# Routing in two halves, routed tiles in the same program as the shared chunks, and the first shared chunk at step 16

## The reference

```python
x = x + xattn(ctx, ctx, layernorm(x), Wv, Wk, Wq, Wo, bo)
x = x + ffn(layernorm(x), ...)

def ffn(x, ...):                      # xf: 2048 x 256
    sh = gelu(einsum('nd,sdh->snh', xf, sw1) + sb1)          # 2 shared experts, 512 wide
    shared_out = (einsum('snh,shd->nd', sh, sw2) + sb2.sum(0)) / 2
    gates = xf @ router_w + router_b                          # 8 experts
    topv, topi = top_k(gates, 2); probs = softmax(topv)
    h = gelu(einsum('nd,edh->enh', xf, w1) + b1)
    y = einsum('enh,ehd->end', h, w2) + b2
    return shared_out + sum over the 2 chosen experts of probs * y
```

## Time and profile before

| | us |
|---|---|
| median of 3 runs (lowest, highest) | 382.54 (381.79, 382.92) |
| the profiled execution | 382.79 |
| its span, first to last instruction | 381.1 |
| PE busy | 332.8 (87%) |
| DVE busy | 234.7 (62%) |
| ACT busy | 222.6 (58%) |
| POOL busy | 201.2 (53%) |
| mean granted clock of PE | 0.957 |

### The profile page before, as it was taken

The page is one execution under the profiler, slowest core; times in us unless marked ns, Lnnn a source line. Parts: engine busy times, 40 slices in busy tenths (PEclk is TensorE's granted clock), DMA queues, the critical chain, the costliest instruction groups (busy, mean ns, idle before and its releaser), DMA issues. The chain is left out here.

```text
span 381.1 us, 8081 instructions
## 1 busy us (share of the span) xinstructions
PE 332.8 (87%) x2297; PEld 279.3 (73%) x2297; DVE 234.7 (62%) x483; ACT 222.6 (58%) x405; POOL 201.2 (53%) x238
## 2 busy tenths in 40 slices
PE   5979989877678999989799658999999999999970
PEld 4757666645457888969689535898999999999860
DVE  0589999999734429694455232565666666566650
ACT  1265567865749646646456414666667676776650
POOL 4326799999737900387377210335554445445542
PEclk9998999998989999999899957999999999999997
DMA  8960000060006201047552643245544544554332
GB/s 267 399 237 1 3 0 31 28 236 0 3 0 233 101 1 57 27 144 211 160 183 88 207 128 135 33 69 85 82 67 78 83 75 72 85 84 63 53 42 28
DMA packets 23929, 36.92 MB, mean 97 GB/s; under 512 B 4400, under 2 KB 18096, under 8 KB 23504
## 3 DMA queue, kind: packets, MB, share of 16 engines
q1 hardware_dynamic: 16000, 25.06, 20.4%
q0 software_dynamic: 7456, 10.04, 15.4%
q10 hardware_dynamic: 432, 1.31, 1.0%
HBM read 23.21 MB, written 13.19 MB: 96 GB/s over the span
## 5 line engine op out<-in xcount | busy, mean ns | idle before, releaser
L945 POOL DMA_INDIRECT out<-y,xg x39 | 61.0, 1564 | 68.6 <-DVE y L1009 51.6
L691 DVE TENSOR_TENSOR h_lo<-g,h_hi 128x512 fp32r<-128x512 f32 x32 | 24.4, 764 | 51.4 <-PE psS L855 26.2
L1063 PE MATMUL ps<-w_lo,hh_hi 128*128 x156 | 47.1, 302 | 3.5 <-DVE hh_lo L1015 3.5
L996 DVE TENSOR_TENSOR hb<-ps,b1T 128x512 f32<-128x512 f32 x39 | 27.0, 691 | 36.5 <-PE ps L1052 36.0
L855 PE MATMUL psS<-s_lo,h_hi 128*128 128x256 f32 x128 | 37.8, 295 | 9.5 <-DVE h_lo L691 9.5
L1063 PE MATMUL ps<-w_hi,hh_lo 128*128 x156 | 44.0, 282 | 0.0
L1063 PE MATMUL ps<-w_hi,hh_hi 128*128 x156 | 43.6, 280 | 0.0
L487 ACT ACTIVATE g<-psP,sb1T 128x512 f32<-128x512 f32 x32 | 22.0, 687 | 34.6 <-PE psP L841 34.5
L381 POOL TENSOR_TENSOR Pr<-Pr,inv 128x1024 f32<-128x1024 f32 x16 | 30.4, 1902 | 19.1 <-DVE inv L682 19.1
L970 ACT ACTIVATE g<-hb 128x512 f32<-128x512 f32 x39 | 24.7, 632 | 26.9 <-DVE hb L996 26.9
L855 PE MATMUL psS<-s_hi,h_lo 128*128 128x256 f32 x128 | 36.9, 288 | 0.0
(11 more groups left out here) (181 smaller groups left out, 913.1 us busy)
## 6 DMA issues: line engine op xcount, KB each, us to landing
wraw<-in_w SPq DMA_DIRECT2D x16, 512.0 KB, 5.7
xg<-xg_d SPq DMA_DIRECT2D x39, 130.0 KB, 2.4
sraw<-in_sw SPq DMA_DIRECT2D x2, 1024.0 KB, 11.0
out<-xres SPq DMA_DIRECT2D x4, 512.0 KB, 3.5
xres<-in_x SPq DMA_DIRECT2D x3, 512.0 KB, 9.5
xTs<-in_xT SPq DMA_DIRECT2D x3, 512.0 KB, 10.1
xg_d<-filler SPq DMA_DIRECT2D x8, 128.0 KB
b_bc<-in_b SPq DMA_DIRECT2D x1, 1024.0 KB, 6.0
```

The costliest lines, as they stand in the source:

```text
L691: V.tensor_tensor(out=h_lo[:, n % 2], in0=g[:, n % 2], in1=h_hi[:, n % 2].bitcast(F32), op=ALU.subtract).then_inc(hlo_done, 1)
L945: pool.indirect_dma_start(out, bass.IndirectOffsetOnAxis(ap=xg[:, t % NXB, D:D + 1].bitcast(U32), axis=0), y[:, t % NYB], None, compute_op ...
L996: V.tensor_tensor(out=hb[:, n % 2], in0=ps[:, 4 + n % 2].rearrange("p (c n) -> p c n", c=HC), in1=b1T[:, bass.ds(e, 1), :].squeeze(1).unsq ...
L1063: last = nc.tensor.matmul(ps[:, 6 + n % 2, 0:D], a[:, n % 2, c], b[:, bass.ds(e, 1), C * HF + c * D:C * HF + (c + 1) * D].squeeze(1), star ...
```

## The change

`front` and `routed_experts` become one function, `program`, with one block of engine programs.

- FIRST_CHUNK is 16. Chunks 0 and 1 stand in the last steps of attention. hidden(n) is now written after output(n-2) in step n, so the order of those two on PE is as before. PE's x2 transposes (L795 before) stand ahead of the Wo product (L788 before) in a step.
- The chunks' hidden parts use two banks of `psS`, the outputs the other two and `psP`. The routed tiles use the chunk's buffers and banks again, with waits on the last chunk's semaphores.
- Routing runs for tiles 0 to 7 (gates at n = 0 and 1, slots at 4) and for tiles 8 to 15 (7, 8 and 11). Tables stand at n = 12 to 14. POOL scatters four groups of eight.
- All low parts are made by DVE, at the n of a table (LOWS), the high parts by ACT at those of HIGHS.
- DVE's additions of a constant to the variance, and the negated mean, are tensor_tensor with a constant column (`eps`, `minus`) in SBUF instead of tensor_scalar with an immediate.
- SP: the store of group 1 comes after expert 5; seven `xg` tiles are loaded ahead of the last stores instead of three.
- `x_transpose(0)` and `(1)` stand at chunks 29 and 30, and the last two outputs between the first routed tiles.

```diff
-FIRST_CHUNK = NT + 2
+FIRST_CHUNK = NT
-EARLY = 3
+EARLY = 7
+SPLIT_X = {5: 1, 10: 2, 18: 3}
+HIGHS = {2: 2, 3: 2, 4: 2, 6: 2, 7: 1, 8: 2, 9: 2, 11: 2, 12: 2, 13: 2, 14: 1, 17: 2, 19: 2, 22: 2, 23: 2, 25: 2, 26: 2}
...
+        h_bank = [psS[:, 0, i] for i in range(2)]
+        y_bank = [psS[:, 1, i, 0:D] for i in range(2)] + [psP[:, i, 0:D] for i in range(2)]
...
 (SP)
-            store(1)
             sp.wait_ge(fill_out, 16 * 2 * NE)
             sp.wait_ge(tabs_ready, 3)
-            sp.wait_ge(slots_ready, 1)
-            sp.wait_ge(lean_done, 1)
+            sp.wait_ge(slots_ready, 2)
+            sp.wait_ge(lean_done, 2)
             sp.wait_ge(fillers, 16 * 7)
             for half in range(2):
                 expert(5, half)
+            store(1)
...
             store(2)
+            sp.wait_ge(y_psum, CHUNKS - HC)
+            sp.dma_start(b2_bc, b2.partition_broadcast(P)).then_inc(b2_in, 16)
+            sp.wait_ge(acc_stored, 16 * 3)
+            tile_in(EARLY)
             store(3)
+            for t in range(NXB, TILES):
+                tile_in(t)
...
 (POOL)
-                if FIRST_CHUNK < s <= FIRST_CHUNK + 4:
-                    for i in range(2):
-                        low(2 * (s - FIRST_CHUNK - 1) + i)
-            weigh(0.5)
-            scatter(0)
-            pool.wait_ge(scattered[0], 16 * NT)
-            weigh(-0.5)
-            scatter(1)
+                if s >= NT + 4:
+                    for t in range(2 * (s - NT - 4), min(2 * (s - NT - 3), HALF_T)):
+                        scatter(0, t)
+            pool.wait_ge(scattered[0][0], 16 * HALF_T)
+            weigh(0, -0.5)
+            for t in range(HALF_T):
+                scatter(1, t)
+            pool.wait_ge(lean_done, 2)
+            weigh(1, 0.5)
+            pool.wait_ge(slots_ready, 2)
...
 (DVE)
-                    V.tensor_scalar(out=ve2[:, t - 1:t + 1], in0=mv2[:, t - 1:t + 1, 1], scalar1=EPS, scalar2=None, op0=ALU.add).then_inc(ve2_done, 1)
-                    V.tensor_scalar(out=nm2[:, t - 1:t + 1], in0=mv2[:, t - 1:t + 1, 0], scalar1=-1.0, scalar2=None, op0=ALU.mult).then_inc(ve2_done, 1)
+                    V.tensor_tensor(out=ve2[:, t - 1:t + 1], in0=mv2[:, t - 1:t + 1, 1], in1=eps[:].to_broadcast([P, 2]), op=ALU.add).then_inc(ve2_done, 1)
+                    V.tensor_tensor(out=nm2[:, t - 1:t + 1], in0=mv2[:, t - 1:t + 1, 0], in1=minus[:].to_broadcast([P, 2]), op=ALU.mult).then_inc(ve2_done, 1)
...
+                    if n == 0:
+                        dve.wait_ge(acc_stored, 16 * NG)
...
 (PE)
+            for t in range(TILES + 2):
+                if t < 2:
+                    shared_out(CHUNKS - 2 + t)
+                if t + 2 < TILES:
+                    x_transpose(t + 2)
...
+                    else:
+                        pe.wait_ge(hhi_done, CHUNKS - 1 + t)
```

More of the change, by code:

```diff
@@ L174, in w_cols, with four, pieces @@
             return t[:, k * PIECE:(k + 1) * PIECE]
+        def four(t):
+            return t.rearrange("p (c n) -> p c n", c=HC)
+        def pieces(table, n):
+            first = sum(k for m, k in table.items() if m < n)
+            return range(first, first + table.get(n, 0))
         def row(t):
@@ L395, in _ @@
+            for t in range(HALF_T, NT):
+                scatter(0, t)
+            pool.wait_ge(scattered[1][0], 16 * HALF_T)
+            weigh(1, -0.5)
             pool.wait_ge(weights_done, 4)
-            scatter(1)
-            for i in range(FREE_ROWS + 1, NE * PPE, 2):
-                low(i)
+            for t in range(HALF_T, NT):
+                scatter(1, t)
             pool.wait_ge(fillers, 16 * 7)
+            pool.wait_ge(tabs_ready, 3)
+            pool.wait_ge(acc_stored, 16 * NG)
@@ L401, in _ @@
+            for i in range(NW):
+                pool.wait_ge(y_out[i], 16 * len(range(i, TILES, NW)))
         @block.scalar
@@ L494, in _ @@
-                    if n % CPG == 4 and n // CPG + 1 < NG:
-                        x_high(n // CPG + 1)
-                    if n == 10:
-                        act.wait_ge(gap_done, 1)
-                        A.activation(lean[:], gap[:], ACT.Tanh, scale=-0.5).then_inc(lean_done, 1)
-                    if n < 4:
-                        for i in range(2 * n, 2 * n + 2):
-                            high(i)
-                    elif 8 <= n < 28:
-                        high(FREE_EARLY + n - 8)
-                    elif n >= 30:
-                        for i in range(2):
-                            high(FREE_ROWS + 2 * (n - 30) + i)
+                    A.activation(h_hi[:, n % 2], h_bank[n % 2], ACT.Gelu, bias=bias).then_inc(hhi_done, 1)
@@ L572, in choose, with indices @@
                     ins = V.max(out=top[:, t], in_=gates[:, t])
                 chain(ins)
-            def indices():
-                for t in range(NT):
+            def indices(h):
+                own = slice(h * HALF_T, (h + 1) * HALF_T)
+                for t in range(h * HALF_T, (h + 1) * HALF_T):
                     ins = V.max_index(out=topi[:, t], in_max=top[:, t], in_values=gates[:, t])
                 chain(ins)
-                V.tensor_tensor(out=gap[:], in0=top[:, :, 1], in1=top[:, :, 0], op=ALU.subtract).then_inc(gap_done, 1)
-                chain(V.tensor_copy(topf[:].rearrange("p k t -> p t k"), topi[:, :, 0:2]))
@@ L588, in one_hot @@
                 chain(ins)
[L589 to L596 removed]
+                V.tensor_tensor(out=ohs[:, own], in0=oh[:, 0, own], in1=oh[:, 1, own], op=ALU.add).then_inc(ohs_ready, 1)
@@ new lines, in gate_rows_out, with shared_out @@
+            def gate_rows_out(h):
+                pe.wait_ge(gt_sb, h + 1)
+                for i in range(HALF_G):
+                    last = T.transpose(gate_rows[h][:, i * P:(i + 1) * P], gT[:, HALF_G * h + i], ident[:])
+                last.then_inc(gates_psum, 1)
+            def shared_out(m):
+                q, e, k = m // CPG, m % CPG // HC, m % HC
+                wc = slice(W1C + k * D, W1C + (k + 1) * D)
+                pe.wait_ge(hlo_done, m + 1)
+                if m == 0:
+                    pe.wait_ge(gt_sb, 1)
+                    pe.wait_ge(gates_read, 1)
+                    pe.wait_ge(pt_sb, NT)
+                for u in range(TPG):
+                    if m % CPG == 0 and q >= 1:
+                        pe.wait_ge(acc_done, TPG * (q - 1) + u + 1)
+                    for i, (a, b) in enumerate(((h_hi, s_lo), (h_lo, s_hi), (h_hi, s_hi))):
+                        last = T.matmul(y_bank[u], a[:, m % 2, u * P:(u + 1) * P], b[:, e, wc],
+                                        start=(m % CPG == 0 and i == 0), stop=(m % CPG == CPG - 1 and i == 2))
+                last.then_inc(y_psum, 1)
@@ new lines, in x_transpose @@
+            def x_transpose(t):
+                pe.wait_ge(xg_in[t % NXB], 16 * (t // NXB + 1))
+                if t == 0:
+                    pe.wait_ge(gates_read, 2)
+                elif t == 1:
+                    pe.wait_ge(slots_ready, 2)
+                else:
+                    pe.wait_ge(x3lo_done, t - 1)
+                for c in range(C):
+                    last = T.transpose(xt_bank[t % 2][:, c * P:(c + 1) * P], xg[:, t % NXB, c * P:(c + 1) * P], ident[:])
+                last.then_inc(xt_psum, 1)
@@ L777, in _ @@
+            for s in range(FIRST_CHUNK + CHUNKS):
                 if s + 1 < NT:
                     scores(s + 1)
+                if 7 <= s < NT + 7:
+                    t = s - 7
+                    pe.wait_ge(rows_done, t + 1)
+                    pe.wait_ge(ot_sb, min(s - 3, NT))
+                    for c in range(C):
+                        last = T.transpose(psA[:, c * P:(c + 1) * P], row(t)[:, c * P:(c + 1) * P], ident[:])
+                    last.then_inc(x2t_psum, 1)
                 if 4 <= s < NT + 4:
```

535 lines of the change are left out of this document (266 added, 269 removed).

## The result

The changed kernel takes **379.93 us** (median of 17 runs, 377.08 to 381.38), the kernel before beside it 383.48 us (17 runs, 381.64 to 386.69): a ratio of 0.990 with an interval of 0.988 to 0.992. It is faster, by 3.6 us; 369.4 was predicted, with a range of 361 to 376. So the sign is right and the size is not.

A forecast was written before the change was run, and what follows sets the result against it. DVE was taken to bound the attention, PE the stretch from step 16 to the last hidden part. 382.8 - 4.6 + 6.0 - 14.5 = 369.7 us, 369.4 as the runs' median; range 361 to 376.

The forecast's parts named there:

- A: The attention: 4.6 us less in all.
- 5.6 us for the form: Attention: tensor_tensor instead of constants on DVE saves half of 11.3 us of waiting, 5.6 us.
- nothing is saved on DVE: Rival, attention: ve and nm each wait for the running POOL instruction; +1.0 there, 375.0 us in all; chance 0.17.
- PE waits for ACT's rows, 1.0 us: Attention: x2 transposes ahead of the Wo product wait for ACT's rows, costing 1.0 us over nine steps.
- B: From step 16 to the last hidden part: 6.0 us more, from five terms.
- (4) and (5): Expert 5's load comes late at chunk 17, PE waits 10.0 us, +7.7; then 3 us at half clock speed, +1.5.
- (1): Chunk 0 begins after tile 14's transposes, chunks 0 and 1 fill PE's idle time: 2.2 us less.
- (3): Ranks stand two and three chunks behind their gates, PE waits for DVE's choice: 2.1 us more with extra instructions.
- (2): PE's four smaller waits for h_lo go, 3.1 us less; DVE's ten added low pieces are hidden.
- The chain of scatters: Slower rival: scatters slow beside DVE's low pieces, delaying expert 7; decides from 1.92 us each, 388.8 at 2.1; chance 0.05.
- C: The passage from the last hidden part to the fourth routed tile: 11.2 us instead of 25.75, 14.5 less.
- Routed tiles and tail: 0: Routed tiles behind the passage are the same work, costed at nothing; nothing was predicted behind the last scatter-add either.

The follow-up runs named there:

- b1_tt: The kernel before with only the tensor_tensor form in place of constants for DVE's small instructions: 383.40 us, ratio 1.001 to the kernel before.
- e5: The changed kernel with DVE's small instructions put back to the form with constants: 378.28 us, ratio 0.988 to the kernel before.
- e6: The changed kernel with DVE's output of a group ahead of the low pieces, in chunks 8, 16, 24: 376.76 us, ratio 0.983 to the kernel before.
- e2_wo_first: The changed kernel with PE's x2 transposes behind the Wo product again: 377.24 us, ratio 0.985 to the kernel before.
- e1_late5: The changed kernel with expert 5's four high pieces in chunks 20 and 21 instead of 17 and 19: 369.48 us, ratio 0.963 to the kernel before.

## Why the prediction was wrong where it was, step by step

**A, "5.6 us for the form": wrong, and the largest error.** Measured: nothing (b1_tt, -0.8 to +1.3 us by its interval). The step argued from the earlier trace rows that a tensor_tensor waits for one POOL instruction and from the earlier trace rows that a tensor_scalar waits for three, and gave the difference to the operation. But the two rows differ in more than the operation: h_lo is 256 times as long as ve, and it came in just as a POOL instruction began. b1_tt puts the new operation at the place of the earlier trace rows, and it waits 3.52 us instead of 3.53. The rival "nothing is saved on DVE" was the right one, though nm did not wait, as it had supposed (it did once, in e5 and e6); its price (375.0) lacked the 3.4 us of the end. The trace of before held the warning: ve itself, in the old form, went in behind one POOL instruction at 97.97, with the next one following at once, and behind two at 63.54 and three at 86.85.

```profile
97.94 1.90 POOL L381 TENSOR_TENSOR Pr<-Pr,inv 128x1024 f32<-128x1024 f32 x1 [1.76 <-DVE inv L682]
97.97 1.90 DVE L654 TENSOR_SCALAR ve<-mv 128x2 f32<-128x2 f32 x1
...
99.81 0.73 POOL L340 TENSOR_TENSOR xres<-xres,sbh 128x256 f32<-128x256 f32 x1
```

So neither the form nor the length decides behind how many it goes in; what does remains open, and no run here was made on it.

**A, "PE waits for ACT's rows, 1.0 us": right in kind, 1.4 measured** (e2_wo_first), 2.7 in the median.

**B (4) and (5), expert 5: right, to a microsecond in sum.** ACT was to wait 10.7 us for the load at chunk 17 and waited 10.95; PE 10.0, and waited 8.56. The clock fell behind it and cost 2.4 where 1.5 were taken. Wait and clock together were to be 7.7 + 2.3 + 1.5 = 11.5 us, and e1_late5 measures 11.0; that it is so near is partly luck, since one part was 1.4 too large and the other 0.9 too small. **(1) to (3)** were to be -3.2 in sum. B as a whole is +4.7; expert 5 makes 11.0 of it, less what the kernel before had in the same place (2.33 of waiting, and 3.4 us at half speed from 188.1, some 1.7), which leaves -2.3. Since B differs by about 2 us between traces, that is no finer test of them. Of (3), 2.1 us, PE's waits ahead of the ranks are 0.8 and 0.7. Of (2), all waits for h_lo but expert 5's have gone, as said; a new one for DVE's output, 2.5 us, was missed: the change moved the output behind the low pieces, and I had costed the low pieces on DVE as hidden.

**The chain of scatters** stayed off the path: with expert 5 in time (e1_late5) PE waits nowhere for expert 7, and a scatter within a group takes 1.44 us from start to start in the mean (1.43 forecast), not 1.92. The four groups took 51 us, from 128.7 to 179.7, where I had 61.7: from one group to the next it was 3.1, 2.5 and 4.1 us from start to start, where I had a scatter and 5.3 more. (The times of two rivals, 366.7 and 388.8, start from the profiled execution's 369.7 and the others from 369.4, a slip of 0.3 us.)

**C: right.** 11.5 us measured, 11.2 forecast; PE's single wait of 0.92 us against "about 0.9"; y(0) began at 231.58, when the last matmul of its result ended (231.26 + 0.28), so it did not wait for the last store.

**"Routed tiles and tail: 0": wrong for the tail.** A block ends with a drain on POOL, and the kernel before hid the first 39 DMAs' share of it in the passage that the change was to close. The change took the drain away there and all of it came back at the end: +3.2 us. I had read the barrier between the blocks as a cost of the passage only, and had not read what the span holds behind the last scatter-add. For the routed tiles themselves 0 stands.

So two steps failed: the 5.6 us of the form, which were 0, and the term of 0 for the tail, which was 3.2. The sign was right since the passage alone gave 14.2 us. Put with these numbers the sum is 382.8 + 1.6 + 4.7 - 14.2 + 3.4 = 378.3, and 2.0 of spread in the routed tiles make 380.3, against 380.2 of the profiled execution; this reads the table once more and is no test of it.
